# A mixing stage: the update of X ahead of the third search, ScalarE's deviation first, the shift on GpSimd

## What is computed

```python
# end of _L0_ffn_ref (H = 256)
moe = jnp.sum(topk_w[..., None] * sel, axis=2)          # two experts' rows per token
y = x + moe
mu = jnp.mean(y, axis=-1, keepdims=True)
var = jnp.var(y, axis=-1, keepdims=True)
return (y - mu) / jnp.sqrt(var + EPS) * gamma + beta    # added to x
# start of _L1_gnn_ref, on the normalised x
h_self = feat @ W_self
h_neigh = feat @ W_neigh
h_sparse = _maxk(h_neigh, 32)                           # keep each row's 32 largest, zero the rest
summed = jax.ops.segment_sum(h_sparse[src], dst, num_segments=n)
```

## Time and profile before

| what | value |
|---|---|
| time before, median of 3 runs | 1418.13 us (1416.08 to 1420.53) |
| the profiled execution | 1423.27 us, span 1421.5 us, mean granted TensorE clock 0.877 |
| PE busy | 1095.9 us (77%) |
| DVE busy | 736.3 us (52%) |
| ACT busy | 624.6 us (44%) |
| POOL busy | 750.7 us (53%) |
| the stage, from its first instruction to its last | about 753 to 928 us of the span |

### The profile page before, as it was taken

One profiled execution on the slowest core, in us unless ns is written; L12 is line 12 of the kernel. 1 busy time (PEld: TensorE's weight loads), 2 busy tenths in 40 slices (PEclk: granted clock), 3 DMA queues, 4 the chain that ended last, 5 costly groups with the idle time before them and its releaser, 6 DMA issues. The chain is left out here.

```text
span 1421.5 us, 27181 instructions
## 1 busy us (share of the span) xinstructions
PE 1095.9 (77%) x7129; PEld 932.3 (66%) x7130; DVE 736.3 (52%) x2453; ACT 624.6 (44%) x1765; POOL 750.7 (53%) x841
## 2 busy tenths in 40 slices
PE   1389899889997379999993777748889887298870
PEld 1378888879996269999991333337767776297660
DVE  7256777776577711111114899845665244733335
ACT  4667666652233324444443555447652012244330
POOL 6677777776500052222215677357767771167770
PEclk9999999999999589999996899965599895589995
DMA  6655555554400379999992222153333342423238
GB/s 196 170 149 150 139 143 144 149 146 128 125 12 19 114 243 350 354 345 358 342 316 91 76 89 87 43 168 108 109 95 116 115 122 66 158 88 98 95 97 275
DMA packets 186770, 220.02 MB, mean 155 GB/s; under 512 B 69103, under 2 KB 148503, under 8 KB 186382
## 3 DMA queue, kind: packets, MB, share of 16 engines
q1 hardware_dynamic: 148240, 125.81, 27.5%
q0 software_dynamic: 32352, 87.30, 20.8%
q10 hardware_dynamic: 6046, 5.40, 1.3%
HBM read 187.33 MB, written 32.19 MB: 154 GB/s over the span
## 5 line engine op out<-in xcount | busy, mean ns | idle before, releaser
L785 POOL DMA_INDIRECT O0G<-n_rows,src_tab x260 | 253.7, 976 | 97.7 <-issue 87.8
L785 POOL DMA_INDIRECT O1G<-sparse_rows,src_tab x188 | 181.4, 965 | 74.2 <-issue 62.1
L804 PE MATMUL O0ps_sums<-O0OH,O0G 128*128 128x80 f32 x1040 | 134.9, 286 | 14.9 <-DVE sumT L840 13.9
L804 PEld LDWEIGHTS O0ps_sums<-O0OH,O0G 128*128 128x128 f32 x1040 | 129.3, 202 | 22.6 <-issue 11.7
L2028 POOL DMA_INDIRECT e0xs<-token_rows,e0idx x60 | 56.7, 945 | 160.1 <-ACT e0idx L2117 156.0
L2168 DVE TENSOR_TENSOR e0ys<-e0ps_y,NR 128x256 f32<-128x256 f32 x64 | 27.2, 425 | 215.5 <-PE e0ps_y L2087 215.5
L804 PEld LDWEIGHTS O1ps_sums<-O1OH,O1G 128*128 128x128 f32 x752 | 117.1, 242 | 21.0 <-issue 18.4
L804 PE MATMUL O1ps_sums<-O1OH,O1G 128*128 128x80 f32 x752 | 118.1, 325 | 15.8 <-issue 11.6
L2073 PE MATMUL e0ps_h<-e0xT,e0W 128*128 128x128 f32 x1024 | 126.4, 277 | 0.9 <-ACT e0xT L2123 0.9
L2073 PEld LDWEIGHTS e0ps_h<-e0xT,e0W 128*128 128x128 f32 x1024 | 120.9, 194 | 1.5 <-issue 1.5
L2087 PE MATMUL e0ps_y<-e0W,e0hidT 128*128 128x256 f32 x512 | 120.9, 379 | 0.0
(11 more groups left out here) (383 smaller groups left out, 2524.8 us busy)
## 6 DMA issues: line engine op xcount, KB each, us to landing
e0W<-in_L_ffn_w SPq DMA_DIRECT2D x128, 512.0 KB, 5.9
O0EA<-in_edge_attr SPq DMA_DIRECT2D x97, 128.0 KB, 2.7
expert_out<-e0ys SPq DMA_DIRECT2D x64, 128.0 KB, 5.2
O0G<-n_rows,src_tab POOLq DMA_INDIRECT x260
e1W_all<-in_L_ffn_w SPq DMA_DIRECT2D x16, 256.0 KB, 5.5
n_rows<-NR SPq DMA_DIRECT2D x5, 640.0 KB
token_rows<-O0N SPq DMA_DIRECT2D x25, 128.0 KB, 2.7
m0own<-token_rows SPq DMA_DIRECT2D x25, 128.0 KB, 2.2
```

Of the source, the lines that this page charges most:

```text
L785: pool.indirect_dma_start(out=self.G[:, s, k, :], out_offset=None, in_=self.rows_dram, in_offset=bass.IndirectOffsetOnAxis(ap=src_tab[:, g ...
L804: last = nc.tensor.matmul(self.ps[o % 2][0:rows.shape[1], half * P:half * P + WINDOW], rows, self.OH[:, h, k, 0:WINDOW], start=(k == 0), s ...
```

## The change

Four moves in `sparse_products`. On VectorE the update of X goes ahead of the third search (r = 2), and the reciprocal of y ahead of the second strike. On ScalarE the deviation of y goes ahead of N3. The shift mr leaves VectorE and is made by GpSimd, as the first thing of its step, ahead of the gathers; there it waits for VectorE's reciprocal of x and for N3 of five tiles before. What is computed stays the same.

```diff
@@ gpsimd
                     def step(at):
+                        if x := at(3):
+                            t, s = x
+                            wait_tile(pool, x_norm.inv, t)
+                            wait_tile(pool, S["n_ready"], t, TU)
+                            nc.gpsimd.tensor_scalar(mr[:, s:s + 1], x_norm.mean(s), x_norm.inverse(s), -1.0,
+                                                    ALU.mult, ALU.mult).then_inc(S["mean_ready"], 1)
                         if x := at(0):
                             mixer.gather(pool, *x)
@@ scalar
+                        if x := at(2):
+                            y_norm.deviation(act, *x)
                         if x := at(3):
                             t, s = x
                             wait_tile(act, S["mean_ready"], t)
                             nc.scalar.activation(N3[:, s, :], tile_of(X, t), ACT.Identity, bias=mr[:, s:s + 1],
                                                  scale=x_norm.inverse(s)).then_inc(S["n_ready"], 1)
-                        if x := at(2):
-                            y_norm.deviation(act, *x)
@@ vector
                         strike(x5, 0)
-                        if x3:
-                            t3, s3 = x3
-                            nc.vector.tensor_scalar(mr[:, s3:s3 + 1], x_norm.mean(s3), x_norm.inverse(s3), -1.0,
-                                                    ALU.mult, ALU.mult).then_inc(S["mean_ready"], 1)
                         if x2:
                             y_norm.join_stats(dve, t, s)
                         largest(x5, 1)
@@
-                        strike(x5, 1)
                         if x2:
                             y_norm.invert(dve, t, s)
-                        largest(x5, 2)
+                        strike(x5, 1)
                         if x2:
                             wait_tile(dve, S["centred"], t)
                             nc.vector.scalar_tensor_tensor(tile_of(X, t), H[:, s, :], y_norm.inverse(s), tile_of(X, t),
                                                            ALU.mult, ALU.add).then_inc(S["x_ready"], 1)
+                        largest(x5, 2)
                         strike(x5, 2)
```

## The result

The changed kernel takes 1430.46 us in the median of 5 runs (1427.21 to 1435.46), the kernel before beside it 1418.41: ratio 1.0081, interval 1.0055 to 1.0107. The forecast was no difference, and the time lies outside the stated range.

What follows compares the result with a forecast made beforehand. VectorE's program in order was taken to bound the 5.96 us step; 17 x (5.91 - 5.96) = -0.9, drain +0.4, fill +0.2, together -0.3 us, gave 1417.8 us against the median of 1418.13, range 1413.8 to 1424.5.

Steps and rivals of the forecast that it cites:

- What bounds the kernel: Steady steps: VectorE's program in order sets the 5.96 us step, 0.47 of it waiting for GpSimd's add.
- The update takes 0.47 once it is ahead of the add: VectorE, steady step: X's update, starting before GpSimd's first add, takes 0.47 us instead of 0.939, saving 0.47 per step.
- Neighbours: VectorE: third search and third strike become adjacent, the strike starting 0.57 us after the search; about +0.22 per step.
- The shift's 0.20 on VectorE is worth nothing: VectorE, between first strike and second search: the shift lies in a wait needed anyway, so removing it gains 0.
- GpSimd's order: GpSimd's step: shift at 0.57 us, gathers at 1.44 (0.60 later than now) and 2.78, product at 5.29 instead of 4.91.
- The loop that makes P = 5.91: Loop across two steps through GpSimd, TensorE, ScalarE and VectorE's reciprocal of y: step P 5.91 us, VectorE waiting 0.20.
- The slower rival: Steady steps: gathers lock the port too, delaying L2394 by 0.37 and X's update by 0.21; P 6.29, 1424.3 us, chance 0.25.
- No term for the clock in the steady part: Steady steps: the TensorE clock was read as granted at 1.00, and the sum held no cost for its falling.
- Low-clock part 0: Steps before the steady part, at low clock: VectorE and GpSimd wait for TensorE there, so the change costs 0.
- Fill and drain: Stage's start and end: fill +0.2 us from later gathers in the fourth step, drain +0.4 from two steps paying for neighbours.

Runs made afterwards that it cites:

- e9: Changed kernel, with GpSimd's first add made to wait until the same step's update of X is done; ratio 1.0025 to the kernel before.
- e4: Changed kernel with the update of X put back behind the third search, the other three moves kept; ratio 1.0078 to the kernel before.
- e2: Kernel before with the shift alone moved to GpSimd, ahead of the gathers; ratio 1.0026 to the kernel before.
- e10: Kernel before, with GpSimd's first add made to wait until the same step's update of X is done; ratio 1.0040.
- first pair: First profiles of the kernel before and the changed kernel, nothing else altered; stage 175.25 us and 184.51 us.
- e8: Changed kernel with one extra 128x512 product per step on TensorE, its result unused; ratio 1.0053 to the kernel before.
- second profile: Changed kernel profiled once more with nothing altered; stage 189.26 us, against 174.17 in the second profile of the kernel before.
- e1: Changed kernel with the shift back on VectorE, all else as changed; ratio 0.9981 to the kernel before.
- e5: Changed kernel with a one-column memset on GpSimd between the second gather and the first add; ratio 1.0071 to the kernel before.
- e7: Changed kernel with the shift on GpSimd placed behind the gathers and ahead of the adds; ratio 1.0028 to the kernel before.

## Why the prediction was wrong, point by point

- **What bounds the kernel: right.** VectorE's order sets the step, and 0.47 of it was the update's wait for the add.
- **The update takes 0.47 once it is ahead of the add: wrong, and this is the step that failed.** It is at the place that I worked out, 3.09 of the step (forecast 3.07 at the earliest), and takes 1.00. I took "ahead of the add" as "starts before the add's record starts". What counts is whether the add stands ready in GpSimd's queue (e9). Measured back from the add's start, in all kernels where it stands ready: updates that start 0.79 us or more ahead of it are free (0.48 to 0.52), those that start 0.18 to 0.71 ahead, 159 of them, are held until about 0.13 ahead of it, as their end less 0.47 shows, and those 0.07 to 0.11 ahead are free again (0.47 to 0.48), thirteen of them, eleven in e4. The prediction had one such row and put it down to the gather: the update at 768.33 ends at 769.24, 0.33 after the start of the add behind (768.92).
- **Neighbours: right.** Third search to its strike 0.56 (884.71 to 885.27), forecast 0.57.
- **The shift's 0.20 on VectorE is worth nothing: right.** First strike to second search is still 0.56 (881.76 to 882.32).
- **GpSimd's order: nearly right.** Shift at 0.58 (forecast 0.57), first gather 0.78 after the shift's start and not 0.87, at 1.36 (1.44), second at 2.72 (2.78). The product is at 5.43 (5.29), since the add is 0.93 long, and nT at 8.02 (7.87).
- **The loop that makes P = 5.91: right as a mechanism, not what binds.** nT at 8.02 gives the reciprocal at 8.61 by the forecast's own terms; VectorE asks for it at 6.27 + 2.35 = 8.62. So the hold has eaten just the time that the loop would have cost. e9 has no hold, though a wait of its own in the loop, and its step of 5.97 to 5.99 is still no gain on 5.96. e2, e4 and e10 show the loop where it does bind.
- **The slower rival (1424.3, chance 0.25) had the size of the step right by coincidence, and the place wrong.** It gave P = 6.29 from 0.37 at the centring and 0.21 at the update; the steady step is 6.27, from 0 and 0.52. Its mechanism, gathers that lock, is refuted by e9. It was also too cheap in all, since it left out the next point.
- **No term for the clock in the steady part: wrong.** ("Low-clock part 0" came out in the first pair: two steps of 14.02 in both. In the second they differ by 1.06, for the clock rose earlier in that profile of before.) In the first profile of the changed kernel the six steps after the rise lose 4.05 us, of which 6 x 0.31 = 1.9 are the hold. The other 2.2 lie in four steps: 1.8 in the three with a relapse, and 0.35 in one of 6.62 with the clock up, whose like stands in e8 (6.60) and in the second profile (6.61) and isn't explained. In the second the twelve steady steps lose 7.6: 3.7 by the hold, 3.2 in the four steps with a relapse, and most of the rest in one step of 6.96 without. I had looked at the clock in the stage before and found 1.00, and didn't ask what a longer idle of TensorE in each step, 1.61 and at times 2.28 instead of 1.30, does to it.
- **Fill and drain: right in sign, small.** Fill +0.5 and +1.0 in the two pairs (forecast +0.2). The two last steps that update X +0.46 (forecast +0.4).

The first pair of profiles adds up: 0.53 to the first search, 0 in the next two steps, 4.05, 3.65 and 1.03 for the rest, 9.26 in all. Left open: how the port is given out inside (that the readiness of the add decides is shown only by taking it away, and no trace shows the port itself), why the hold ends just ahead of the add, what besides the idle decides on a relapse, and why they are more in one execution than in another. No version here is faster than before beyond its interval; the best, e1, is at 0.9981 (0.9956 to 1.0006).

## What to carry to other kernels

When a VectorE instruction with two SBUF inputs is moved away from a GpSimd one, look at what stands in GpSimd's queue at that time, not only at what runs: an add that waits for nothing but its turn behind a gather holds VectorE as if it ran. A small instruction put at the head of an engine's step is priced by what queues behind it: the shift takes 0.27 us there, but it moved two gathers by 0.5 and used up the slack of a loop over two steps. And a change that lengthens TensorE's idle between bursts can bring the low clock back, so look for it in the windows.

## What the hardware did that I had not expected

- An update that is held behind a gather ends 0.32 to 0.35 us after the queued add's start, and that add is then 0.90 to 0.94 us long instead of 0.72 to 0.75; so their records overlap partly. An update that starts within 0.11 us ahead of the add isn't held at all (e4).
- The hold is there also with a memset (e5) or a one-column instruction (e7) between gather and add, and gone when the add has to wait for the update (e9).
- Behind the one-column shift a gather starts 0.78 us after the shift's start in the steady steps, though the shift takes only 0.27.
- The clock can fall to 1.2 GHz and come back after 3.4 us in the midst of a steady loop, seven times in one stage.
